# A two-layer attention and mixture kernel: row maxima by 32-row matmuls over four PSUM banks, and another order of two TensorE steps

## The reference

```python
x = x + _L0_xattn_ref(_layernorm(x), ctx, ctx, ...)      # 16 heads of 16
x = x + _L0_ffn_ref(_layernorm(x), ...)                  # expert choice
x = x + _L1_xattn_ref(_layernorm(x), ctx, ctx, mask, pad_mask, ...)
x = x + _L1_ffn_ref(_layernorm(x), ...)                  # 8 experts, all used

# attention, per batch b and head h
attn = einsum('bhqd,bhkd->bhqk', Q, K) / sqrt(16)
attn = where(mask[q, k], attn, -1e8)                     # layer 1 only
attn = where(pad_mask[b, k], attn, -1e8)                 # layer 1 only
out = softmax(attn) @ V
```

## Time and profile before

| | |
|---|---|
| median of 3 runs | 2528.04 us (2525.23 to 2528.23) |
| the profiled execution | 2527.97 us, of which its span 2526.4 us |
| PE busy | 2272.7 us (90%), 14663 instructions |
| PEld (weight loads) | 1960.2 us (78%) |
| DVE / ACT / POOL busy | 1462.2 / 861.7 / 464.8 us |
| mean granted TensorE clock | 0.953 |
| attention 0, its loop | about 72 to 490 us of the span |
| attention 1, its loop | about 980 to 1420 us |
| last mixture | 1420 to 2526 us |

### The profile page before, as it was taken

How to read it: one execution, slowest core, us unless ns; L and a number is a source line. 1 busy time by engine, 2 the same in 40 slices (tenths; PEclk the granted TensorE clock), 3 DMA queues, 4 the chain that set the end, 5 groups by cost and what they waited for, 6 DMA issues and landing times. The chain is left out here.

```text
span 2526.4 us, 39469 instructions
## 1 busy us (share of the span) xinstructions
PE 2272.7 (90%) x14663; PEld 1960.2 (78%) x14663; DVE 1462.2 (58%) x3129; ACT 861.7 (34%) x1210; POOL 464.8 (18%) x413
## 2 busy tenths in 40 slices
PE   5888888565899976999999599999999999999999
PEld 3677777543788874877877588888888888888888
DVE  5777777475554526767776485545454545454444
ACT  1454544202444422444444342222222222222222
POOL 3122222200666542222221220000000000000000
PEclk8999999775899997999999799999999999999999
DMA  2021211200444330111211310000000000000000
GB/s 71 26 75 50 75 50 59 73 4 23 108 97 94 65 45 23 68 58 56 69 50 43 127 32 26 25 26 26 26 26 26 26 26 26 26 25 26 24 9 11
DMA packets 117497, 114.85 MB, mean 45 GB/s; under 512 B 15440, under 2 KB 114320, under 8 KB 117392
## 3 DMA queue, kind: packets, MB, share of 16 engines
q1 hardware_dynamic: 105104, 96.29, 12.0%
q0 software_dynamic: 12288, 17.05, 4.1%
HBM read 62.72 MB, written 50.59 MB: 45 GB/s over the span
## 5 line engine op out<-in xcount | busy, mean ns | idle before, releaser
L1802 DVE TENSOR_TENSOR zmix_hid<-zmix_act_gate,psum 128x1024 f32<-128x1024 f32 x128 | 156.3, 1221 | 389.8 <-issue 359.3
L143 PE MATMUL psum<-zmix_wd_hi,zmix_hid_hi 128*128 128x256 f32 x1024 | 289.6, 283 | 1.9 <-DVE zmix_acc L1793 1.7
L145 PE MATMUL psum<-zmix_wd_hi,zmix_hid_lo 128*128 128x256 f32 x1024 | 290.1, 283 | 0.0
L144 PE MATMUL psum<-zmix_wd_lo,zmix_hid_hi 128*128 128x256 f32 x1024 | 290.0, 283 | 0.0
L1746 ACT ACTIVATE zmix_act_gate<-psum 128x1024 f32<-128x1024 f32 x128 | 131.8, 1029 | 403.2 <-PE psum L145 403.2
L1754 ACT ACTIVATE zmix_hid_hi<-zmix_hid 128x1024 fp32r<-128x1024 f32 x128 | 135.5, 1059 | 383.8 <-PE psum L145 285.7
L593 PEld LDWEIGHTS psum<-att_v_cur,att_probs 128*128 128x128 f32 x2048 | 247.4, 193 | 9.5 <-ACT att_probs L693 3.6
L593 PE MATMUL psum<-att_v_cur,att_probs 128*128 128x96 f32 x2048 | 247.2, 275 | 2.7 <-ACT att_probs L693 2.7
L1807 DVE TENSOR_TENSOR zmix_hid_lo<-zmix_hid,zmix_hid_hi 128x1024 fp32r<-128x1024 f32 x128 | 158.7, 1240 | 135.1 <-ACT zmix_hid_hi L1754 134.2
L143 PE MATMUL psum<-zmix_xT_hi,zmix_wg_hi 128*128 128x512 f32 x512 | 203.3, 397 | 12.0 <-DVE zmix_xT_lo L1782 12.0
L1793 DVE SCALAR_TENSOR_TENSOR zmix_acc<-psum,zmix_weight,zmix_acc 128x256 f32<-128x256 f32 x512 | 211.8, 476 | 1.6 <-PE psum L145 1.6
(11 more groups left out here) (285 smaller groups left out, 4754.3 us busy)
## 6 DMA issues: line engine op xcount, KB each, us to landing
x<-att_x_new SPq DMA_DIRECT2D x32, 512.0 KB, 2.9
att_x_in<-in_x SPq DMA_DIRECT2D x16, 512.0 KB, 3.8
rows<-att_normed_new SPq DMA_DIRECT2D x16, 512.0 KB, 3.0
att_x_in<-x SPq DMA_DIRECT2D x16, 512.0 KB, 3.9
normed<-att_normed_new SPq DMA_DIRECT2D x16, 512.0 KB, 2.9
zmix_xn<-normed SPq DMA_DIRECT2D x16, 512.0 KB, 4.7
zmix_acc<-x SPq DMA_DIRECT2D x16, 512.0 KB, 4.4
out_x<-zmix_acc SPq DMA_DIRECT2D x16, 512.0 KB, 3.2
```

The lines of the kernel that those rows point to most:

```text
L143: pe.matmul(out, st_hi, mv_hi, start=first, stop=False)
L144: pe.matmul(out, st_hi, mv_lo, start=False, stop=False)
L145: return pe.matmul(out, st_lo, mv_hi, start=False, stop=last)
L1802: dve.tensor_tensor(hid[:, :, :], act_gate[:, :, :], psum[:, 2:4, :], ALU.mult).then_inc(up_out, 1)
```

## The change

Maxima on TensorE are now made per chunk, all four tiles at once, over the four banks 2 to 5. Bank 2+j takes head pair j: for each tile one matmul of 32 rows, 128 tokens as weights, 2x64 columns of the pair's own keys. A chunk has 16 of them where there were 4 of 128 rows and 512 columns. The second chunk waits until the first is fully reduced. Chunk 0 follows values of tile 0, chunk 1 those of tile 2. VectorE's reductions read 4 banks with the same 512 elements each, still two after each tile. `kb_hi` and `kb_lo` keep 2 copies of the keys (even head, odd head; `evenodd` in place of `headmask`) instead of 8, made in two GpSimd operations instead of four.

The mask is added to the maxima by an identity matmul per bank (128 rows, 512 columns) of a token-side mask, `mask_tok`, which VectorE makes anew for each batch; in the scores the mask matmuls have 64 rows, alternately of the lower and upper half. For this the masks are loaded and cast in a second form. `turn_attention` now stands ahead of `turn_maxima`.

```diff
-    ident, headmask, negsel, keysel = const["ident"], const["headmask"], const["negsel"], const["keysel"]
+    ident, evenodd, negsel, keysel = const["ident"], const["evenodd"], const["negsel"], const["keysel"]
...
-    keyf = sc.sb("keysel_f", [P, H // 2, SK])
+    keyf = sc.sb("keysel_f", [P, 2, SK])
...
+        pool.tensor_tensor(half_sums[:, :], headmask[:, 0:HH // 2], headmask[:, HH // 2:HH], ALU.add).then_inc(made, 1)
+        pool.wait_ge(made, 8 + PAIR_ROWS)
+        pool.tensor_tensor(evenodd[:, :], half_sums[:, 0:2], half_sums[:, 2:4], ALU.add).then_inc(made, 1)
...
+        pool.tensor_copy(const["ident16"][:, :], ident[:, :]).then_inc(made, 1)
...
-            sp.dma_start(mask32[:, :], w["mask"]).then_inc(mask_loaded, 16)
-            sp.dma_start(pad32[:, :], w["pad"]).then_inc(mask_loaded, 16)
-            sp.wait_ge(mask_loaded, 32)
+            for a in range(2):
+                sp.dma_start(mask32[a * SK:(a + 1) * SK, :], w["mask"]).then_inc(mask_loaded, 16)
+                sp.dma_start(pad32[a * SK:(a + 1) * SK, :], w["pad"]).then_inc(mask_loaded, 16)
+            sp.dma_start(rows32[:, :, :], w["mask_rows"].rearrange("(t p) k -> p t k", p=P)).then_inc(mask_loaded, 16)
+            sp.dma_start(pads32[:, :, :].rearrange("p b k -> p (b k)"), w["pad_rows"].partition_broadcast(P)).then_inc(mask_loaded, 16)
+            sp.wait_ge(mask_loaded, 96)
...
+            dve.tensor_scalar(kv["mask_rows"][:, :, :], rows32[:, :, :].bitcast(U8), BIG, -BIG, ALU.mult, ALU.add)
+            dve.tensor_scalar(kv["pad_rows"][:, :, :], pads32[:, :, :].bitcast(U8), BIG, -BIG, ALU.mult, ALU.add)
...
-            if masked:
-                pool.memset(mask_cur[:, :, :], 0.0).then_inc(cleared, 1)
...
-                for c in range(KC):
-                    for out, k in ((kb_hi, kv["kT_hi"]), (kb_lo, kv["kT_lo"])):
-                        cols = k[:, c, bass.ds(b * SK, SK)].bitcast(F32).unsqueeze(1).to_broadcast([P, HH, SK])
-                        pool.tensor_tensor(out[:, p, c, :, :], cols, hm, ALU.mult).then_inc(kb_ready, 1)
+                own = const["evenodd"][:, :].unsqueeze(1).unsqueeze(3).to_broadcast([P, KC, 2, SK])
+                for out, k in ((kb_hi, kv["kT_hi"]), (kb_lo, kv["kT_lo"])):
+                    cols = k[:, :, bass.ds(b * SK, SK)].bitcast(F32).unsqueeze(2).to_broadcast([P, KC, 2, SK])
+                    pool.tensor_tensor(out[:, p, :, :, :], cols, own, ALU.mult).then_inc(kb_ready, 1)
...
-            def maxima(b, p, tiles):
-                if 0 in tiles:
+            def maxima(b, p, c):
+                if c == 0:
                     pe.wait_ge(q_hi, done(KC, b, KC))
...
-                    after(pe, exp_done, done(NP, b - 1, PAIR_ROWS + 2))
+                    after(pe, exp_done, done(NP, b - 1, NP))
                     if masked:
-                        pe.wait_ge(mask_ready, b + 1)
-                for t in tiles:
-                    for c in range(KC):
-                        after(pe, s_taken, done(TT * KC, b, t * KC + c - 1))
-                        m = pe.matmul(psum[:, 2 + c, :], qT_hi[:, p, c, t * P:(t + 1) * P], kb_hi[:, p, c, :, :],
-                                      start=True, stop=not masked)
-                        if masked:
-                            m = pe.matmul(psum[:, 2 + c, :], mask_cur[:, p, t * P:(t + 1) * P], const["keysel"][:, :, :],
-                                          start=False, stop=True)
-                        m.then_inc(s_made, 1)
+                        pe.wait_ge(mask_ready, done(2, b, 2))
+                else:
+                    pe.wait_ge(s_taken, done(TT * KC, b, c * TT))
+                if masked:
+                    for j in range(PAIR_ROWS):
+                        pe.matmul(psum[:, 2 + j, :], const["ident16"][:, :],
+                                  mask_tok[:, p, :, :].unsqueeze(2).to_broadcast([P, TT, 2, SK]), start=True, stop=False)
+                for t in range(TT):
+                    for j in range(PAIR_ROWS):
+                        rows = slice(j * ROWS, (j + 1) * ROWS)
+                        m = pe.matmul(psum[:, 2 + j, t * P:(t + 1) * P], qT_hi[rows, p, c, t * P:(t + 1) * P],
+                                      kb_hi[rows, p, c, :, :], start=not masked, stop=not masked or t == TT - 1)
+                m.then_inc(s_made, 1)
...
-                    for out, rows, heads in quarters:
-                        pe.matmul(out, const["keysel"][:, 0:2, :], mask_cur[:, p, :], start=False, stop=True).then_inc(st_made, 1)
+                    for j, (out, rows) in enumerate(quarters):
+                        keys = slice(j % 2 * SK, (j % 2 + 1) * SK)
+                        pe.matmul(out, const["keysel"][keys, :, :], mask_cur[keys, p, :], start=False, stop=True).then_inc(st_made, 1)
...
                 for t in range(TT):
                     weighted_values(b, p, t)
-                    if nxt:
-                        maxima(b + 1, 1 - p, [t])
+                    if nxt and t % 2 == 0:
+                        maxima(b + 1, 1 - p, t // 2)
...
+                turn_attention(b)
                 if nxt:
                     turn_maxima(b + 1)
-                turn_attention(b)
...
-            maxima(0, 0, range(TT))
+            for c in range(KC):
+                maxima(0, 0, c)
...
+                pads = kv["pad_rows"][:, bass.ds(b, 1), :].to_broadcast([P, TT, SK])
+                dve.tensor_tensor(mask_tok[:, p, :, :], kv["mask_rows"][:, :, :], pads, ALU.min).then_inc(mask_ready, 1)
...
                 for t in tiles:
-                    for c in range(KC):
-                        dve.wait_ge(s_made, done(TT * KC, b, t * KC + c + 1))
-                        s = psum[:, 2 + c, :].rearrange("p (j a k) -> p j a k", a=2, k=SK)
-                        dve.tensor_reduce(s_max[:, t, :, 2 * c:2 * c + 2], s, AX.X, ALU.max).then_inc(s_taken, 1)
+                    s = psum[:, 2:2 + PAIR_ROWS, t * P:(t + 1) * P].rearrange("p j (a k) -> p j a k", a=2)
+                    dve.tensor_reduce(s_max[:, t, :, 2 * c:2 * c + 2], s, AX.X, ALU.max).then_inc(s_taken, 1)
...
                     if nxt:
-                        maxima(b + 1, [t])
+                        maxima(b + 1, t // 2, [2 * (t % 2), 2 * (t % 2) + 1])
```

More of the change, by code:

```diff
@@ L403, in attention @@
         mask_cur = sc.sb("mask_cur", [P, 2, S], BF16) if masked else None
+        mask_tok = sc.sb("mask_tok", [P, 2, TT, SK], BF16) if masked else None
         x_loaded = [sc.sem(f"x_loaded{p}") for p in range(2)]
@@ L564, in scores @@
                     pe.wait_ge(exp_done, done(NP, b, c * PAIR_ROWS))
-                quarters = [(psum[:, 2 + j, :], slice(j * ROWS, (j + 1) * ROWS), slice(2 * j, 2 * j + 2)) for j in range(PAIR_ROWS)]
-                for out, rows, heads in quarters:
-                    pe.matmul(out, kb_hi[rows, p, c, heads, :], qT_hi[rows, p, c, :], start=True, stop=False)
-                for out, rows, heads in quarters:
-                    pe.matmul(out, kb_hi[rows, p, c, heads, :], qT_lo[rows, p, c, :], start=False, stop=False)
-                for out, rows, heads in quarters:
-                    pe.matmul(out, kb_lo[rows, p, c, heads, :], qT_hi[rows, p, c, :], start=False, stop=False)
-                for out, rows, heads in quarters:
+                quarters = [(psum[:, 2 + j, :], slice(j * ROWS, (j + 1) * ROWS)) for j in range(PAIR_ROWS)]
+                for out, rows in quarters:
+                    pe.matmul(out, kb_hi[rows, p, c, :, :], qT_hi[rows, p, c, :], start=True, stop=False)
+                for out, rows in quarters:
+                    pe.matmul(out, kb_hi[rows, p, c, :, :], qT_lo[rows, p, c, :], start=False, stop=False)
+                for out, rows in quarters:
+                    pe.matmul(out, kb_lo[rows, p, c, :, :], qT_hi[rows, p, c, :], start=False, stop=False)
+                for out, rows in quarters:
                     m = pe.matmul(out, const["negsel"][rows, c, :], maxT[rows, :], start=False, stop=not masked)
@@ L626, in route @@
                 m.then_inc(lg_made, 1)
-            pe.wait_ge(cleared, 3 if masked else 2)
+            pe.wait_ge(cleared, 2)
             def body(b, p, half):
@@ L876, in _ @@
             queries_lo(0, 0)
-            maxima(0, range(TT))
+            for c in range(KC):
+                maxima(0, c, range(TT))
             maxima_copy(0)
@@ L1885, in two_layers @@
             kv = alloc_layer(Scope(nc, layer, "att0"), False)
-            first_setup(nc, const, kv, layer_weights("0", mask=None, pad=None), psum)
+            first_setup(nc, const, kv, layer_weights("0", mask=None), psum)
             attention(nc, const, kv, psum, a["x"], x1_by_batch, rows1.rearrange("(b s) r -> b s r", s=S)[:, :, 0:D], logits)
```

37 lines of the change are left out of this document (23 added, 14 removed).

## The result

The changed kernel takes 2517.79 us (median, 2511.96 to 2520.59), the kernel before beside it 2528.46 (2525.23 to 2530.63): ratio 0.9957, 95% interval 0.9944 to 0.9969. It is faster by 10.7 us; the forecast was 22.3. Direction and range held, the size was off by a factor of two.

A forecast was written before the change was run, and what follows sets the result against it. Each attention transition was taken as bound by a chain through TensorE, ACT and VectorE. Unmasked -9.9, masked -9.9, starts -6.5 +2.9 and choice stage +1.1 gave -22.3, so 2505.7 us, range 2499 to 2532.

The forecast's parts named there:

- unmasked first half: Unmasked attention, scores to transposes of the normed rows: TensorE arrives some 1.5 us before ACT, so a gain of 0.
- unmasked second half: Unmasked attention, transposes of the normed rows to next scores: -0.87 for order, +0.21 for new maxima, sum -0.66 a transition.
- unmasked loop, whole: All 15 transitions of the unmasked attention stage at -0.66 each: -9.9 us.
- masked, a transition: Masked attention, one batch to the next: first half -0.51 with ACT last, second half -0.15, sum -0.66.
- start, first statistics to first scores: Ahead of each loop: less GpSimd work releases small VectorE operations, -3.0 and -3.5; later first maxima, +1.1 and +1.8.
- choice stage: VectorE chain of the choice stage: two added operations for the masks' other form, +1.1 us.
- clock: TensorE's granted clock: no drop in the sum, so 0; a drop behind longer waits was left to rival E.
- The groups of four: Maxima on TensorE: four 32-row matmuls of 128 columns take 0.109 us together, so one chunk costs 0.75.
- Rival B: Maxima on TensorE: a group of four small matmuls takes 0.23, total about 2526; chance 0.22.
- rival C: Maxima on TensorE: small matmuls of different row groups don't overlap, kernel slower at 2565; chance 0.12.
- The swap: Second halves: attended rows ahead of turned maxima fit into VectorE's reductions, -0.87 a transition in both stages.
- rival E: Unmasked stage: longer TensorE waits ahead of L663 drop the clock, +1 in each of 15 transitions, 2521; chance 0.04.

## Why the prediction was right and wrong

Point by point, of the profiled execution:

| step | forecast | measured |
|---|---|---|
| unmasked first half | 0 | 0 (15.1 to 15.2) |
| unmasked second half, a transition | -0.66 | -0.57 (the 8 short ones) |
| unmasked loop, whole | -9.9 | -7.8 without the falls; +2.0 as it ran |
| masked, a transition | -0.66 | -0.75 |
| masked loop, whole | -9.9 | -9.8 |
| start, first statistics to first scores | -1.9 and -1.7 | -2.8 (30.7 to 27.9) and -1.2 (31.8 to 30.6) |
| choice stage | +1.1 | +0.8 |
| clock | 0 | 6 falls of 1.63: +9.8 |

Without the last line the measured parts come to -20.8, with it to -11.0; the medians differ by 10.7. (The profiled execution was another 5 us shorter, in set-up and mixture stretches that differ by as much between runs with the same code there. It was also the fastest of the six, with the highest mean clock, 0.949 against 0.944 to 0.946: by an estimate from 5.5 us at 1.63 each, the common execution has some three falls more.) In the unmasked loop 14 transitions give 0.57 each. The first, which begins at the lower clock, gives nothing: from the first scores to the first L663 it took 36.71 before and 36.94 now, at mean clocks of 0.95 and 0.91.

The groups of four: right. 0.11 was taken; the loads of the sixteen start in groups of four at 209.00, 209.11, 209.22 and 209.33, and the sixteen take 0.60 between neighbours, 0.67 with their tail. Rival B (0.23) and rival C (one by one) are out; the run with one row group has C's price, 1.93 a chunk, where C was walked out at 2.05. In the unmasked second half the sum had 0.75 for a chunk against 0.54 of the old form, +0.21; measured it is +0.31 (9.75 against 9.44 of the swap alone). It is the one price of the loops that was too low, by 0.1. Beside the swap alone, the step into the small matmuls costs 0.14 more (1.85 and 1.71 from values to maxima), they themselves 0.05 more, and the values behind them 0.10 more until VectorE can start (2.06 and 1.96). The reductions over four banks, which were priced at nothing, took 1.28 a pair as before.

The swap: right, -0.87 measured as -0.87 in both stages.

The masked sum: right as a total, its halves -0.62 and -0.13 (forecast -0.51 and -0.15). That L680 would still wait for ACT was near the mark: ACT ends the norm at 1091.04, TensorE's transposes start at 1091.19 with no idle time shown.

The start: near as a sum of the two stages (-3.6 forecast, -4.0 measured), too small in one and too large in the other. The unmasked start varies from 27.9 to 29.5 between kernels with the same code there, -1.2 to -2.8, so this nearness is partly luck. The cause that it rested on, GpSimd holding small VectorE operations, is what the later GpSimd work shows.

The step that failed is the clock, which the sum put at nothing and left to rival E. The prediction saw the mechanism (it says that the longer waits ahead of L663 might drop the clock, priced 1 in each of 15 transitions, 2521) and then gave it 0.04, because waits of 1.0 and 1.5 in the kernel before had gone with a clock of 1.00. Those were two separate waits. The change takes away the 1.00 ahead of the maxima of tile 1, TensorE comes to L663 earlier, and one wait of 1.57 to 1.73 stands there; this was in the working ("TensorE gets to L663 some 1.5 us before ACT") and was booked as 0 since ACT sets the end. The idle time of a transition hardly changed (1.00 and 1.51 before, 1.71 and 0.81 now), only where it lies. A wait that costs nothing by itself cost 1.63 behind it, in 6 of 14 transitions: rival E's price was too low by 0.63 and its count of 15 too high by 9. Filling that wait took every one of these falls away. Rival E's 2521 came nearer to 2517.8 than the forecast did, by two errors that partly cancel.

A second thing the prediction's own numbers showed and it didn't say: of its sum of -22.3, -26.1 (30 times 0.87) is the swap, and all the rest together is +3.8. The maxima, the main part of the change, were forecast to lose in the unmasked second half, and they did.

## What to carry over

When an edit moves TensorE's short waits together into one longer wait, price the stretch behind it at the lower clock as well, even where another engine ends the chain. Here that was 1.63 each time it happened. Then look whether ready work queued behind the wait (here the values of the next tile) can go in front of it. Price each part of a composite change by itself before adding up: here a swap of two steps carried more than the total. A new form of an operation that removes a wait is worth that wait only in a stretch whose length its own engine sets; elsewhere the wait turns up again further on.

## What the runs showed that was not expected

- The granted clock fell to the lower level behind single waits of 1.57 to 1.73, with TensorE busy 89% of the first half around them (13.5 of 15.2 us), in 6 of 14 nearly equal transitions. With a wait of 1.61 to 1.73 and one of 2.00 it fell in 13 of 13; where the first of the two was 0.85 it did not, and with the one of 2.00 alone (masked) it fell in 4 of 14. Which transition is hit is not told by the length of its wait: 1.71 stood ahead of a short half and 1.57 ahead of a long one. What decides was not found.
- It also fell with no wait at all, behind sixteen 32-row matmuls on one row group that took 1.93 one after another, while the rows call TensorE busy for 2.00 of each 2.00 us.
- The order in which 32-row matmuls of four row groups are issued made no difference over sixteen of them: four in a row on the same rows, 0.63; in turn, 0.60; all on one group, 1.93. It fits row groups that work off their own matmuls independently; no run shows more than sixteen.
- Small VectorE operations (128x8, 0.17) took up to 2.26 beside a GpSimd tensor operation, to its end. Holding GpSimd back by one wait took 4.0 and 5.4 us off the two starts.
